# A gather of 32 per loop turn shared between GpSimd and SyncE in a graph-network kernel on one Trainium2 core

## The chip, the cores and the metric

The kernel runs on one core of one Trainium2 chip. Its time is the device time of one execution in microseconds (us). Before the change it is 2132.71 us, the median of three runs (2131.5 to 2132.8).

The engines are TensorE (PE, with its weight loads as PEld), VectorE (DVE), ScalarE (ACT), GpSimd (POOL) and SyncE (SP). SP computes nothing here: it waits on semaphores and issues DMA transfers. POOL issues the gathers, that is, DMA transfers whose source rows are named by a list of indices.

## The reference

A layer of a graph network with 6250 nodes and 206250 edges, sorted by destination. Each node has 160 values: 64 scalars and 32 vectors of three.

```python
h = jnp.maximum(_layernorm(x, axis=-1), 0.0)
# inside the layer, with node_input = h:
h = relu(edge_length_embedded @ W_fc1 * (1/sqrt(10))) * RELU_GAIN
w = h @ W_fc2 * (1/sqrt(100))                    # weights of each edge
l0, l1 = _fctp_scalar_attr(x0, x1, a, W_l1_0, W_l1_1)
y0 = l0[edge_src]; y1 = l1[edge_src]             # the gather
m0 = w0 * y0 * e0
m1 = (w1 * y0)[:, :, None] * e1[:, None, :]
m2 = (w2 * e0)[:, :, None] * y1
m3 = w3 * einsum('eud,ed->eu', y1, e1) * INV_SQRT3
s0..s3 = segment_sum(m0..m3, edge_dst)           # sum over the edges of a node
out = si + 0.5 * (products of s0..s3 with W_l2_*)
x = x + out
```

## The kernel before, in words

**Node stage (0 to some 80 us).** The nodes are normalized and multiplied by the first weights, and SP stores the result as `table` in HBM, one row of 160 float32 (640 bytes) for each node (line 239).

**Edge stage (86 to some 2120 us).** The edges are cut into 403 groups of T = 4 tiles of P = 128 edges. Per group:

- POOL gathers 128 rows of `table` for each of the four tiles into a row buffer `y[:, j]` (line 361), so 4 gathers a group and 1612 in all. There are G = 4 row buffers. Before it writes one it waits until DVE has finished with the group that used it four groups ago (`msg_done`, line 357).
- PE computes the hidden values of the edges (`fc1`, L823), ACT takes the relu (L459), and PE computes the edge weights (`fc2`, L830).
- DVE makes the one-hot matrix `hot` (L647), waits for the group's rows (line 650), multiplies the vectors by the attributes (`dots`, L620), scales `hot` (L654), sums the dots (L624), and makes the messages from rows and weights (L630, L635, L640). L640 is the last of a group's messages: it brings `msg_done` to 4 per group.
- PE sums the messages over the edges of each destination (`windows`, L858 and L860), and DVE adds the result into `acc` (L682).

The hardware loop runs over pairs of turns, that is 8 groups or 32 gathers; there are 50 pairs (`PAIRS`) and 3 groups after them. In each pair one block of 128 nodes is finished besides (PE L836 to L848, DVE L667), and its rows are stored by SP (line 254).

**What SP does in the edge stage.** `load_half` (lines 263 to 277) loads, for every two groups, the radial inputs `rad` (10 x 1024, waits for `fc1_done`, line 266), the indices `idx` (128 x 8, waits until the gathers that used the old ones have landed, line 271), and the attributes `attr_sb` (128 x 32, waits for `msg_done`, line 275). That is 12 transfers in a pair, issued strictly one after another: what stands behind a wait on SP waits too. A transfer whose address is in a register needs small register instructions ahead of it (FUSED_REGOPS or ALU_OP, and MOVE), which the trace shows on the queue of SP.

Nothing but these semaphores orders POOL, SP, DVE, ACT and PE against each other.

Of the kernel before, what the change touches and what calls it, by code (L numbers as in the profile page):

```python
# [6 lines left out]
P = 128  # L7
N = 6250
E = 206250
MUL0, MUL1 = 64, 32  # L10
C = MUL0 + 3 * MUL1
# [3 lines left out]
CHUNK = 7  # L15
CHUNKS = BLOCKS // CHUNK
assert CHUNKS % 2
STORES = CHUNKS + 1
# [6 lines left out]
NP = BLOCKS * P  # L25
# [12 lines left out]
assert TURNS == 2 * PAIRS + 1  # L38
LAG = 3

IN_LOOP = PAIRS - LAG
# [22 lines left out]

def gnn_layer(nc, x, src, dst, radial, attr, avec, w_lin, w_lin_z, w_self, w_self_z, w_last, wf1, wf2, out):
    ctx = ExitStack()
    with ctx:
        def sb(name, shape, dt=F32):
            return ctx.enter_context(nc.sbuf_tensor(name, shape, dt))

        def sem(name):
            return ctx.enter_context(nc.semaphore(name))
# [61 lines left out]
        idx_sum = sb("idx_sum", [P, 1], I32)  # L134
        rows_in = y[:, 0, :, :].rearrange("p t c -> p (t c)")[:, 0:4 * P]

# [37 lines left out]
        ld_rad = [sem(f"ld_rad{c}") for c in range(2)]  # L174
        gathered = [sem(f"gathered{j}") for j in range(G)]
        fc1_done = sem("fc1_done")
# [43 lines left out]
        def _(sp):  # L220
# [41 lines left out]

            def load_half(i, c, first):
                k = i * 2 + c
                if not first:
                    sp.wait_ge(fc1_done, (k - 1) * HALF)
                    sp.sem_inc(sp_passed, 1)
                sp.dma_start(rad[:, c, :], radial[:, bass.ds(k * HALF * GE, HALF * GE)]).then_inc(ld_rad[c], 16)
# [4 lines left out]
                sp.dma_start(idx[:, c, :], src[:, bass.ds(k * HALF * T, HALF * T)]).then_inc(ld_idx[c], 16)  # L273
# [3 lines left out]
                sp.dma_start(attr_sb[:, c, :, :], attr[:, bass.ds(k * HALF * T, HALF * T), :]).then_inc(ld_attr[c], 16)  # L277

            def windowed():
                for c in range(2):  # L280
                    load_half(0, c, True)

                half_way = TURNS // 2
                with sp.Fori(1, half_way) as i:
                    for c in range(2):
                        load_half(i, c, False)
                early = (half_way // 2 - LAG - 1) // CHUNK
                for c in range(early):
                    store_out(c, 0, CHUNK)
                with sp.Fori(half_way, TURNS) as i:  # L290
                    for c in range(2):
                        load_half(i, c, False)
                store_rest(early)

            def general():

                sp.wait_ge(zeroed, 1)
                with sp.Fori(0, ND // P) as b:
                    sp.dma_start(sums_d[bass.ds(b * P, P), :], acc[:, 0, 0:4 * P]).then_inc(g_zeroed, 16)
                with sp.Fori(0, GROUPS) as g:  # L300
                    sp.wait_ge(g_free, g + 1)
                    sp.sem_inc(sp_passed, 1)
                    sp.dma_start(rad[:, 0, 0:GE], radial[:, bass.ds(g * GE, GE)]).then_inc(g_loaded, 16)
                    sp.dma_start(idx[:, 0, 0:T], src[:, bass.ds(g * T, T)]).then_inc(g_loaded, 16)
                    sp.dma_start(attr_sb[:, 0, 0:T, :], attr[:, bass.ds(g * T, T), :]).then_inc(g_loaded, 16)
                sp.wait_ge(g_turn, TILES + 1)
                with sp.Fori(0, BLOCKS) as b:
                    sp.wait_ge(g_block_free, b + 1)
                    sp.sem_inc(sp_passed, 1)
                    sp.dma_start(rows_in, sums_d[bass.ds(b * P, P), :]).then_inc(g_block_in, 16)  # L310
                store_rest(0)
# [6 lines left out]
        def _(pool):  # L318
# [33 lines left out]

            def gather_group(i, j, first):
                if j % HALF == 0:
                    pool.wait_ge(ld_idx[j // HALF], i * 16 + 16)
                if not first:
                    pool.wait_ge(msg_done, (i * G + j - G + 1) * 4)
                    pool.sem_inc(pool_passed, 1)
                for t in range(T):
                    col = (j % HALF) * T + t  # L360
                    nc.gpsimd.indirect_dma_start(  # L361
                        out=y[:, j, t, :], out_offset=None, in_=table,
                        in_offset=bass.IndirectOffsetOnAxis(ap=idx[:, j // HALF, col:col + 1], axis=0),
                    ).then_inc(gathered[j], 16)

            def windowed():
                for j in range(G):
                    gather_group(0, j, True)
                with pool.Fori(1, TURNS - 1) as i:  # L369
                    for j in range(G):  # L370
                        gather_group(i, j, False)

                for j in range(LEFT):
                    gather_group(TURNS - 1, j, False)

# [141 lines left out]
        def _(dve):  # L517
# [96 lines left out]

            def attr_of(j, a, b):
                return attr_sb[:, j // HALF, (j % HALF) * T:(j % HALF) * T + T, a:b]

            def edge_dots(j):

                nc.vector.tensor_tensor(dots[:, :, :, :], vectors(j), attr_of(j, 1, 4).unsqueeze(3).to_broadcast([P, T, 3, MUL1]),  # L620
                                        ALU.mult).then_inc(dots_done, 1)
# [19 lines left out]

            def messages(i, j):
                g, s = i * G + j, j % 2
                if j % HALF == 0:
                    dve.wait_ge(ld_attr[j // HALF], i * 16 + 16)
# [4 lines left out]
                dve.wait_ge(gathered[j], i * (16 * T) + 16 * T)  # L650
                edge_dots(j)
                dve.wait_ge(hot_done, g + 1)

                nc.vector.tensor_tensor(hot[:, s, :, 1:V, :], hot[:, s, :, 0:1, :].to_broadcast([P, T, 4, W]),  # L654
                                        attr_of(j, 0, 4).unsqueeze(3).to_broadcast([P, T, 4, W]), ALU.mult).then_inc(msg_done, 1)
                dve.wait_ge(dots_done, g + 1)
                sum_dots()
                dve.wait_ge(fc2_done, g + 1)
                scalar_products(j, s)
                vector_products(j, s)  # L660
                dve.wait_ge(dot_done, g + 1)
                dot_products(s)
# [24 lines left out]
            def windowed():  # L687
                def pair(k, first, last_of_block):
                    for j in range(2 * G):
                        g = k * (2 * G) + j  # L690
                        messages(k * 2 + j // G, j % G)
# [9 lines left out]
                for j in range(LEFT):  # L701
                    g = (TURNS - 1) * G + j
                    messages(TURNS - 1, j)
                    accumulate(g - 1, (g - 1) % 2, base_of(g - 1), False)
# [6 lines left out]
            def general():  # L711
# [4 lines left out]
                with dve.Fori(0, GROUPS) as g:  # L716
                    dve.wait_ge(g_loaded, g * 48 + 48)
                    dve.wait_ge(g_rows, g * (16 * T) + 16 * T)
                    edge_dots(0)
                    dve.drain()  # L720
# [50 lines left out]
        def _(pe):  # L771
# [130 lines left out]
            def general():  # L902
# [15 lines left out]
                with pe.Fori(0, BLOCKS) as b:  # L918
                    pe.wait_ge(g_block_in, b * 16 + 16)
                    for v in range(4):  # L920
                        ins = nc.tensor.transpose(ps_w[:, 0, v, 0:P], rows_in[:, v * P:(v + 1) * P], ident[:, :])
                    ins.then_inc(g_block_turned, 1)
# [71 lines left out]
```

## Time and profile before

| | |
|---|---|
| median of three runs | 2132.71 us (2131.5 to 2132.8) |
| the profiled execution | 2139.31 us |
| its span, first to last instruction | 2137.5 us |
| mean granted TensorE clock | 0.928 of full speed |
| busy shares | PE 95%, PEld 75%, DVE 79%, POOL 74%, ACT 16% |
| gathers | 1612, first at 86.0 us, last at 2117.7 us |
| DMA | 158.29 MB, 74 GB/s over the span |

Busy means that an instruction runs; a gather's busy time is POOL's time to issue it, not the time that the data takes. "Idle before" is time in which an engine had nothing running, and the releaser is what ended it; "issue" is idle time in which it waited for nothing that the profile shows. Names with a q (SPq, DVEq) are the instruction queues of the engines. The profiled execution is 6.6 us longer than the median.

### The profile page before, as it was taken

How to read it: one execution, taken by the hardware profiler on the slowest of the kernel's cores; microseconds unless marked ns; L12 is line 12 of the kernel's file. 1: busy time of each engine (PE TensorE's matmuls, PEld its weight loads, DVE VectorE, ACT ScalarE, POOL GpSimd, SP SyncE). 2: the span in 40 equal slices, each digit the busy share in tenths (PEclk: the TensorE clock that was granted, in tenths of full speed). 3: DMA queues.
4: the chain of work that ended last, by engine and by line, in shares of the span. 5: the costliest groups of instructions: out<-in, count | busy, mean ns of one | idle time of the engine just before them, and what ended most of it. 6: DMA issues, size and time to landing. Idle time of an engine off the chain costs nothing.

```text
span 2137.5 us, 42022 instructions
## 1 busy us (share of the span) xinstructions
PE 2021.8 (95%) x11466; PEld 1603.7 (75%) x11466; DVE 1684.6 (79%) x4634; ACT 343.0 (16%) x636; POOL 1576.3 (74%) x1637
## 2 busy tenths in 40 slices
PE   6899999999999999999999999999999999999998
PEld 5677777787778778777777777777777777777776
DVE  6478878788787888888877888887888878888786
ACT  4311111111111111111111111111111111111111
POOL 6277777777777777777777777777777777777774
PEclk8699999899998998999998989999999989998998
DMA  4223222223222332232232223233232322322233
GB/s 134 72 70 72 72 72 70 71 71 72 71 72 69 71 72 71 70 73 71 71 103 71 71 71 71 72 71 72 71 71 71 73 70 70 73 72 69 71 72 91
DMA packets 159932, 158.29 MB, mean 74 GB/s; under 512 B 86882, under 2 KB 131846, under 8 KB 159914
## 3 DMA queue, kind: packets, MB, share of 16 engines
q0 software_dynamic: 77376, 132.16, 25.0%
q1 hardware_dynamic: 81400, 24.49, 5.2%
q10 hardware_dynamic: 1138, 1.43, 0.2%
q8 instruction: 8, 0.13, 0.0%
q14 instruction: 10, 0.08, 0.0%
HBM read 149.90 MB, written 8.03 MB: 74 GB/s over the span
## 4 chain that ended last, share of the span: by engine, by line
POOL 31%; issue 25%; DMA 18%; DVE 15%; PE 9%; DVEq 1%; POOLq 1%; ACT 0%; SPq 0%; ACTq 0%
POOL y L361 31%; DMA y<-table,idx 17%; DVE hot L654 5%; DVE msg L630 5%; DVE dot L624 4%; PE ps_s L858 2%; PE ps_w L830 2%; PE ps_s L860 2%; PE ps_h L823 1%; DVE dots L620 1%; PE ps_w L792 1%; DVE stats L520 1%; PE ps_h L781 0%; POOLq L369 0%; DVEq L685 0%
## 5 line engine op out<-in xcount | busy, mean ns | idle before, releaser
L361 POOL DMA_INDIRECT y<-table,idx x1612 | 1541.9, 957 | 536.5 <-issue 490.5
L830 PEld LDWEIGHTS ps_w<-w_fc,hr 100*128 100x128 f32 x3224 | 539.3, 197 | 331.8 <-issue 331.8
L830 PE MATMUL ps_w<-w_fc,hr 100*128 100x192 f32 x3224 | 663.0, 351 | 0.0
L858 PE MATMUL ps_s<-hot,msg 128*128 128x128 f32 x3224 | 485.0, 298 | 67.9 <-DVE msg L640 67.3
L858 PEld LDWEIGHTS ps_s<-hot,msg 128*128 128x128 f32 x3224 | 436.6, 206 | 112.3 <-DVE msg L640 109.0
L459 ACT ACTIVATE hr<-ps_h 100x512 f32<-100x512 f32 x403 | 240.7, 597 | 1681.1 <-PE ps_h L823 1681.1
L823 PE MATMUL ps_h<-rad,w_fc 10*100 10x512 f32 x806 | 464.1, 656 | 5.7 <-DMA rad<-in_radial 5.7
L620 DVE TENSOR_TENSOR dots<-y,attr_sb 128x384 f32<-128x384 f32 x403 | 225.1, 559 | 276.7 <-DMA y<-table,idx 276.3
L860 PE MATMUL ps_s<-hot,msg 128*128 128x64 f32 x3224 | 432.0, 280 | 0.0
L860 PEld LDWEIGHTS ps_s<-hot,msg 128*128 128x128 f32 x3224 | 423.3, 205 | 0.0
L682 DVE TENSOR_TENSOR acc<-acc,ps_s 64x32 f32 (+1 forms) x1612 | 325.2, 202 | 71.6 <-PE ps_s L860 31.1
L630 DVE TENSOR_TENSOR msg<-ps_w,y 128x512 f32<-128x512 f32 x403 | 278.4, 691 | 21.1 <-PE ps_w L830 8.6
L654 DVE TENSOR_TENSOR hot<-hot,attr_sb 128x512 f32<-128x512 f32 x403 | 275.3, 683 | 0.0
L624 DVE TENSOR_REDUCE dot<-dots 128x128 f32<-128x384 f32 x403 | 235.8, 585 | 0.0
L635 DVE TENSOR_TENSOR msg<-ps_w,y 128x384 f32<-128x384 f32 x403 | 220.3, 547 | 0.0
L647 DVE TENSOR_TENSOR hot<-iota_w,dst_rel 128x128 f32<-128x128 f32 x403 | 117.8, 292 | 19.1 <-DMA attr_sb<-in_attr 6.2
L823 PEld LDWEIGHTS ps_h<-rad,w_fc 10*100 10x100 f32 x806 | 103.1, 166 | 35.5 <-DMA rad<-in_radial 5.8
L640 DVE TENSOR_TENSOR msg<-ps_w,dot 128x128 f32<-128x128 f32 x403 | 112.7, 280 | 0.0
L421 ACT ACTIVATE hid<-xres,shift,rstd 128x160 f32 (+1 forms) x98 | 47.9, 510 | 3.7 <-DVE shift L535 3.7
L781 PE MATMUL ps_h<-ident,hid 128*128 128x128 f32 x49 | 19.1, 396 | 23.9 <-ACT hid L421 23.9
L667 DVE SCALAR_TENSOR_TENSOR xres<-ps_s,a_sb,xres 128x160 f32 x47 | 17.7, 377 | 24.5 <-PE ps_s L860 24.1
L842 PE MATMUL ps_s<-w_out,fin_in 128*128 128x160 f32 x94 | 25.0, 350 | 12.8 <-DVE msg L640 12.8
(79 smaller groups left out, 527.0 us busy)
## 6 DMA issues: line engine op xcount, KB each, us to landing
y<-table,idx POOLq DMA_INDIRECT x1612
rad<-in_radial SPq DMA_DIRECT2D x202, 40.0 KB
xres<-in_x SPq DMA_DIRECT2D x7, 560.0 KB, 4.2
table<-y SPq DMA_DIRECT2D x6, 560.0 KB, 3.2
out<-xres SPq DMA_DIRECT2D x6, 560.0 KB, 4.7
idx<-in_src SPq DMA_DIRECT2D x202, 4.0 KB
attr_sb<-in_attr SPq DMA_DIRECT2D x202, 16.0 KB
dst_i<-in_dst ACTq DMA_DIRECT2D x1, 808.0 KB, 6.3
```

What stands on the lines that cost most here:

```text
L361: nc.gpsimd.indirect_dma_start(out=y[:, j, t, :], out_offset=None, in_=table, in_offset=bass.IndirectOffsetOnAxis(ap=idx[:, j // HALF, col ...
L459: nc.scalar.activation(hr[:, s, :], ps_h[0:N_RADIAL, s, 0:GE], ACT.Relu, scale=K_RADIAL).then_inc(relu_done, 1)
L620: nc.vector.tensor_tensor(dots[:, :, :, :], vectors(j), attr_of(j, 1, 4).unsqueeze(3).to_broadcast([P, T, 3, MUL1]), ALU.mult).then_inc(do ...
L624: nc.vector.tensor_reduce(dot[:, :, :], dots[:, :, :, :].rearrange("p t d u -> p t u d"), AX.X, ALU.add).then_inc(dot_done, 1)
L630: nc.vector.tensor_tensor(msg[:, s, :, 0:2 * MUL0].rearrange("p t (k u) -> p t k u", k=2), ps_w[:, s, :, 0:2 * MUL0].rearrange("p t (k u) ...
L635: nc.vector.tensor_tensor(msg[:, s, :, 2 * MUL0:M - MUL1].rearrange("p t (d u) -> p t d u", d=3), ps_w[:, s, :, 2 * MUL0:NW - MUL1].unsque ...
L654: nc.vector.tensor_tensor(hot[:, s, :, 1:V, :], hot[:, s, :, 0:1, :].to_broadcast([P, T, 4, W]), attr_of(j, 0, 4).unsqueeze(3).to_broadcas ...
L682: nc.vector.tensor_tensor(to, to, p[rows, cols].rearrange("p (v n) -> p v n", n=W), ALU.add).then_inc(acc_done, 1)
L823: nc.tensor.matmul(ps_h[0:N_RADIAL, j % 2, 0:GE], w_fc1[:, :], rad[:, j // HALF, (j % HALF) * GE:(j % HALF + 1) * GE], start=True, stop=Tr ...
L830: ins = nc.tensor.matmul(ps_w[:, s, t, 0:NW], hr[:, s, t * P:(t + 1) * P], w_fc2[:, :], start=True, stop=True)
L858: nc.tensor.matmul(ps_s[:, s, 0:4 * W], msg[:, s, t, 0:P], hot[:, s, t, 1:V, :], start=(t == 0), stop=(t == T - 1))
L860: ins = nc.tensor.matmul(ps_s[:, s, 4 * W:6 * W], msg[:, s, t, P:M], hot[:, s, t, 0:2, :], start=(t == 0), stop=(t == T - 1))
```

## The change

Of the 32 gathers of a pair, the last (group 7 of the pair, tile 3) is shared. POOL gathers its first 64 rows only. The other 64 rows are fetched by SP, one transfer of 640 bytes for each, whose source address comes from a register. SP first loads the 64 indices into one partition (`idx_row`, one transfer in a pair, from a copy of `src` in another layout), and loads registers from there in four batches of 16.

A fifth row buffer is added: group 7 of a pair uses buffer 4, so groups 3 and 7 now have a buffer each that is used once in a pair. Indices and attributes are loaded for four groups at once instead of two (4 transfers in a pair instead of 8), the radial inputs as before (4). SP's order of work in a pair is written out by hand in `step`. The rows of group 7 may be written once DVE has finished all groups of the pair before (`msg_done` at k times 32), and DVE waits for four more semaphores (`rows_in`) at group 7.

```diff
+ROWS = 64
+BATCH = 16
+BATCHES = ROWS // BATCH
+APART = 2 * G - 1
+
+def slot_of(p, j):
+    return G if p * G + j == APART else j
...
-        idx = sb("idx", [P, 2, HALF * T], I32)
-        attr_sb = sb("attr_sb", [P, 2, HALF * T, 4])
+        idx = sb("idx", [P, 2, G * T], I32)
+        attr_sb = sb("attr_sb", [P, 2, G * T, 4])
-        y = sb("y", [P, G, T, C])
+        y = sb("y", [P, G + 1, T, C])
+        idx_row = sb("idx_row", [1, ROWS], I32)
...
+            def load_idx(k, p, first):
+                i = k * 2 + p
                 if not first:
-                    for j in range(HALF * c, HALF * c + HALF):
-                        sp.wait_ge(gathered[j], i * (16 * T))
+                    for j in range(G):
+                        sp.wait_ge(gathered[p * G + j], k * (16 * T))
                     sp.sem_inc(sp_passed, 1)
+                sp.dma_start(idx[:, p, :], src[:, bass.ds(i * G * T, G * T)]).then_inc(ld_idx[p], 16)
+
+            def load_attr(k, p, first):
+                i = k * 2 + p
                 if not first:
-                    sp.wait_ge(msg_done, (k - 1) * HALF * 4)
+                    sp.wait_ge(msg_done, (i - 1) * (4 * G))
...
+            def load_row_idx(k):
+                tile = k * (2 * G * T) + 2 * G * T - 1
+                sp.dma_start(idx_row[:, :], src_row[bass.ds(tile, 1), P - ROWS:P]).then_inc(ld_row, 16)
+
+            def fetch_rows(k, q):
+                _, nodes = nc.values_load_multi_w_load_instructions(
+                    idx_row[0:1, q * BATCH:(q + 1) * BATCH], engines=[sp.engine], min_val=0, max_val=NP - 1, ...)
+                for r, node in enumerate(nodes):
+                    at = P - ROWS + q * BATCH + r
+                    sp.dma_start(y[at:at + 1, G, T - 1, :], table[bass.ds(node, 1), :]).then_inc(rows_in[q], 16)
+
+            def step(k, first):
+                load_idx(k, 1, first)
+                sp.wait_ge(ld_row, k * 16 + 16)
+                if not first:
+                    sp.wait_ge(msg_done, k * (8 * G))
+                    sp.sem_inc(sp_passed, 1)
+                fetch_rows(k, 0)
+                load_attr(k, 1, first)
+                load_rad(k * 2 + 1, 0, False)
+                fetch_rows(k, 1)
+                load_rad(k * 2 + 1, 1, False)
+                load_idx(k + 1, 0, False)
+                fetch_rows(k, 2)
+                load_attr(k + 1, 0, False)
+                load_rad(k * 2 + 2, 0, False)
+                fetch_rows(k, 3)
+                load_rad(k * 2 + 2, 1, False)
...
+                def steps(lo, hi):
+                    with sp.Fori(lo, hi) as k:
+                        load_row_idx(k)
+                        step(k, False)
...
+            def gather_group(k, p, j, first):
+                if j == 0:
+                    pool.wait_ge(ld_idx[p], k * 16 + 16)
+                n = p * G + j
                 if not first:
-                    pool.wait_ge(msg_done, (i * G + j - G + 1) * 4)
+                    held = 2 * G if n in (G - 1, APART) else G
+                    pool.wait_ge(msg_done, (k * (2 * G) + n - held + 1) * 4)
                     pool.sem_inc(pool_passed, 1)
                 for t in range(T):
+                    rows = P - ROWS if n == APART and t == T - 1 else P
                     nc.gpsimd.indirect_dma_start(
-                        out=y[:, j, t, :], ...
+                        out=y[0:rows, slot_of(p, j), t, :], ...
                     ).then_inc(gathered[n], 16)
...
+                n, at = p * G + j, slot_of(p, j)
+                dve.wait_ge(gathered[n], k * (16 * T) + 16 * T)
+                if n == APART:
+                    for q in range(BATCHES):
+                        dve.wait_ge(rows_in[q], k * (16 * BATCH) + 16 * BATCH)
+                edge_dots(p, j)
```

The lines that are not shown rename variables and pass the pair and its half instead of the turn.

## Rows read from the trace of the kernel before

**Rows 1.** The page, part 1: busy time of each engine.
```profile
PE 2021.8 (95%) x11466; PEld 1603.7 (75%) x11466; DVE 1684.6 (79%) x4634; ACT 343.0 (16%) x636; POOL 1576.3 (74%) x1637
```

**Rows 2.** One line, the gathers (L361): nanoseconds least/median/most; idle by releaser.
```profile
L361 POOL DMA_INDIRECT y<-table,idx x1612: 942/946/1456, 86.0 to 2117.7; - x180
...
  issue: 490.5, 1461
  DVE msg L630: 43.9, 144
...
  DVE dots L620: 276.3, 338
```

**Rows 3.** Timeline, 2085 to 2091 us: start, length, engine, line, operation.
```profile
2085.14 0.95 POOL L361 DMA_INDIRECT y<-table,idx  x1 [0.30 <-issue]
2085.23 0.56 DVE L620 TENSOR_TENSOR dots<-y,attr_sb 128x384 f32<-128x384 f32 x1 [0.77 <-DMA y<-table,idx]
...
2086.39 0.95 POOL L361 DMA_INDIRECT y<-table,idx  x1 [0.30 <-issue]
...
2088.00 0.28 DVE L640 TENSOR_TENSOR msg<-ps_w,dot 128x128 f32<-128x128 f32 x1
...
2090.31 0.56 DVE L620 TENSOR_TENSOR dots<-y,attr_sb 128x384 f32<-128x384 f32 x1 [0.89 <-DMA y<-table,idx]
```

**Rows 4.** Busy time of engines by stretch; then clock, DMA share, GB/s.
```profile
300.00:1000.00 700.00, 675.11 (x3831) 533.04 (x3830) 565.62 (x1546) 105.82 (x191) 530.96 (x556) 0.93 0.30 71
1080.00:1090.00 10.00, 10.00 (x39) 8.33 (x37) 5.62 (x15) 0.60 (x1) 7.56 (x8) 0.52 0.83 243
```

**Rows 5.** Timeline, 1080 to 1094 us, with a low clock.
```profile
1080.24 2.48 SPq L254 DMA_DIRECT2D out<-xres  x3
...
1083.14 1.21 SPq L268 DMA_DIRECT2D rad<-in_radial  x1
...
1088.99 0.56 DVE L620 TENSOR_TENSOR dots<-y,attr_sb 128x384 f32<-128x384 f32 x1 [2.99 <-DMA y<-table,idx]
```

**Rows 6.** Waits of the queue of SP: total us, times, longest.
```profile
SPq L272 <- DMA y<-table,idx: 1056.2, 200, 10.3
SPq L276 <- DVE msg L640: 543.8, 200, 6.4
```

**Rows 7.** Lines 268, 273, 277 on SP (three answers): nanoseconds least/median/most.
```profile
L268 SPq DMA_DIRECT2D rad<-in_radial x202: 312/312/1208, 80.9 to 2099.1; - x101
L268 SPq FUSED_REGOPS  x200: 52/58/71, 86.7 to 2098.9; - x100
...
L273 SPq DMA_DIRECT2D idx<-in_src x202: 347/352/377, 81.4 to 2105.5; - x101
...
L277 SPq DMA_DIRECT2D attr_sb<-in_attr x202: 332/333/433, 81.8 to 2108.6; - x101
```

**Rows 8.** Line 277 on SP: what runs in 1009.36 to 1009.37 us.
```profile
L277 SPq ALU_OP  x1: 33/33/33, 1009.4 to 1009.4; - x1
```

**Rows 9.** Timeline on SP, 1009.4 to 1010.0 us.
```profile
1009.49 0.33 SPq L277 DMA_DIRECT2D attr_sb<-in_attr  x1
```

**Rows 10.** Timeline on SP, 81 to 84 us: transfers back to back.
```profile
81.37 0.38 SPq L273 DMA_DIRECT2D idx<-in_src  x1
81.78 0.42 SPq L277 DMA_DIRECT2D attr_sb<-in_attr  x1
...
82.66 0.35 SPq L273 DMA_DIRECT2D idx<-in_src  x1
```

**Rows 11.** Loads of registers: line 685 (DVE), line 211 (SP).
```profile
L685 DVEq TENSOR_LOAD <-base_i x403: 299/305/1010, 99.2 to 2128.2; - x135
...
L211 SPq TENSOR_LOAD <-flag_i x1: 477/477/477, 79.6 to 79.6; - x1
```

**Rows 12.** The chain that ended last, 80 to 90 us: start, length, what.
```profile
81.37 1.69 DMA idx<-in_src
```

More of the change, by code:

```diff
@@ L134, in gnn_layer @@
         idx_sum = sb("idx_sum", [P, 1], I32)
-        rows_in = y[:, 0, :, :].rearrange("p t c -> p (t c)")[:, 0:4 * P]
+        sums_in = y[:, 0, :, :].rearrange("p t c -> p (t c)")[:, 0:4 * P]
         def ps(name, shape):
@@ L174, in gnn_layer @@
         ld_rad = [sem(f"ld_rad{c}") for c in range(2)]
-        gathered = [sem(f"gathered{j}") for j in range(G)]
+        gathered = [sem(f"gathered{j}") for j in range(2 * G)]
+        ld_row = sem("ld_row")
+        rows_in = [sem(f"rows_in{q}") for q in range(BATCHES)]
         fc1_done = sem("fc1_done")
@@ new lines, in load_row_idx @@
+            def load_row_idx(k):
[3 more added lines that the diff above has]
+                _, nodes = nc.values_load_multi_w_load_instructions(
+                    idx_row[0:1, q * BATCH:(q + 1) * BATCH], engines=[sp.engine], min_val=0, max_val=NP - 1,
+                    skip_runtime_bounds_check_because="src names rows of x, as in the reference's own gather")
+                for r, node in enumerate(nodes):
+                    at = P - ROWS + q * BATCH + r
+                    sp.dma_start(y[at:at + 1, G, T - 1, :], table[bass.ds(node, 1), :]).then_inc(rows_in[q], 16)
@@ L279, in windowed @@
             def windowed():
+                load_idx(0, 0, True)
+                load_row_idx(0)
+                load_attr(0, 0, True)
                 for c in range(2):
[L281 to L287, printed above, removed]
+                    load_rad(0, c, True)
+                sp.wait_ge(table_out, 16 * STORES)
@@ L288, in windowed @@
+                step(0, True)
+                half_way = PAIRS // 2
+                def steps(lo, hi):
+                    with sp.Fori(lo, hi) as k:
+                        load_row_idx(k)
+                        step(k, False)
+                steps(1, half_way)
+                early = (half_way - LAG - 1) // CHUNK
                 for c in range(early):
                     store_out(c, 0, CHUNK)
-                with sp.Fori(half_way, TURNS) as i:
-                    for c in range(2):
-                        load_half(i, c, False)
+                steps(half_way, PAIRS)
@@ L351, in _ @@
             pool.wait_ge(table_out, 16 * STORES)
-            def gather_group(i, j, first):
-                if j % HALF == 0:
-                    pool.wait_ge(ld_idx[j // HALF], i * 16 + 16)
+            def gather_group(k, p, j, first):
+                if j == 0:
+                    pool.wait_ge(ld_idx[p], k * 16 + 16)
+                n = p * G + j
                 if not first:
-                    pool.wait_ge(msg_done, (i * G + j - G + 1) * 4)
+                    held = 2 * G if n in (G - 1, APART) else G
+                    pool.wait_ge(msg_done, (k * (2 * G) + n - held + 1) * 4)
                     pool.sem_inc(pool_passed, 1)
                 for t in range(T):
-                    col = (j % HALF) * T + t
+                    rows = P - ROWS if n == APART and t == T - 1 else P
                     nc.gpsimd.indirect_dma_start(
-                        out=y[:, j, t, :], out_offset=None, in_=table,
-                        in_offset=bass.IndirectOffsetOnAxis(ap=idx[:, j // HALF, col:col + 1], axis=0),
-                    ).then_inc(gathered[j], 16)
+                        out=y[0:rows, slot_of(p, j), t, :], out_offset=None, in_=table,
+                        in_offset=bass.IndirectOffsetOnAxis(ap=idx[0:rows, p, j * T + t:j * T + t + 1], axis=0),
+                    ).then_inc(gathered[n], 16)
             def windowed():
-                for j in range(G):
-                    gather_group(0, j, True)
-                with pool.Fori(1, TURNS - 1) as i:
+                for p in range(2):
                     for j in range(G):
-                        gather_group(i, j, False)
+                        gather_group(0, p, j, p == 0 or j == G - 1)
+                with pool.Fori(1, PAIRS) as k:
+                    for p in range(2):
+                        for j in range(G):
+                            gather_group(k, p, j, False)
                 for j in range(LEFT):
-                    gather_group(TURNS - 1, j, False)
+                    gather_group(PAIRS, 0, j, False)
             def general():
@@ L690, in pair @@
                         g = k * (2 * G) + j
-                        messages(k * 2 + j // G, j % G)
+                        messages(k, j // G, j % G)
                         if j >= 1 or not first:
@@ L702, in windowed @@
                     g = (TURNS - 1) * G + j
-                    messages(TURNS - 1, j)
+                    messages(PAIRS, 0, j)
                     accumulate(g - 1, (g - 1) % 2, base_of(g - 1), False)
```

43 lines of the change are left out of this document (21 added, 22 removed).

## The prediction

> **What bounds the kernel now.** I read the busy shares first. PE looks like the bound at 95% and POOL has 74% [rows 1], but a busy share doesn't say who waits. So the next view is the line of the gathers: POOL issues 1612 of them between 86.0 and 2117.7 us, each 0.946 us long, and the idle time before them is "issue", 490.5 us in 1461 cases, or 0.34 us each with the start left in; the 144 cases put down to DVE come to 43.9 us, 0.30 us each [rows 2]. The timeline shows the same 0.30 us before gathers that waited for nothing, so those 144 are no waits either [rows 3]. POOL is therefore never held up: it starts one gather every 1.25 us, 2085.14 to 2086.39 [rows 3], and on average every (2117.7 - 86.0) / 1611 = 1.261 us [rows 2]. A pair of 32 gathers takes 40.36 us, and 50 pairs are nearly the whole span. DVE waits for gathered rows 338 times, 276.3 us in all [rows 2], and its groups start 5.08 us apart [rows 3].
>
> PE is the bound only for short stretches. The mean clock is 0.93, and in 1080 to 1090 us it is 0.52 [rows 4], close to the lower level of 1.2 GHz, after a stretch in which PE had small gaps. DVE starts its next group late there, 2.99 us idle [rows 5], but POOL stays at 7.56 us busy in those 10 us, the same share as elsewhere [rows 4]: the row buffers cover it. So less time on POOL shortens the whole, if what replaces it fits beside.
>
> **What the change removes.** 50 times, half of one gather. With 128 rows it costs 0.946 us [rows 2]. No gather with fewer rows is in the trace. The bounds: nothing saved (all fixed cost), and half, 0.473 us (all by row). A negative value has no reason, as POOL does the same with fewer rows. The only row there is gives the cost with all rows and shows no fixed part except the 0.30 us between gathers, which stays; I take three quarters of the upper end, 0.355 us, an estimate. Saved: 50 x 0.355 = 17.7 us, ends 0 and 23.7. POOL's pair becomes 40.0 us.
>
> The Trainium skill (DMA: Bandwidth & Descriptors, Anatomy of one DMA) says of descriptor generation that "You can emit a lot of descriptors before the incremental cost shows up". By that sentence the saving is 0 and the sum is 2132.7; no row here shows it either way.
>
> **What it adds on SP.** 64 transfers of one row in a pair. SP issues one after another, so this is a sum. Nearest row for a transfer with a register address: line 277 starts its first register instruction by 1009.36 [rows 8], its transfer at 1009.49 for 0.33 us [rows 9], and back to back there are about 0.045 us until the next (81.37 + 0.38 is followed at 81.78, with 0.03 us) [rows 10]. That is 0.13 + 0.33 + 0.045 = 0.505 us. The transfer itself takes 0.352 and 0.333 us with 128 rows and 0.312 with 10 [rows 7]; with one row I take 0.30, an estimate on that slope, so 0.475 us for each. Upper end: 0.352 plus 0.145 and 0.045, 0.542. Lower end: 0.30 with register instructions that overlap half, 0.41. Transfers behind a large one take longer (0.42 us for attributes behind indices), behind a small one not (0.35 for indices behind the radial load) [rows 10]; rows are small. Registers: four loads of 16. One load of one value takes 0.305 us on DVE and 0.477 on SP [rows 11]; if a batch is one load, 1.2 to 1.9 us in a pair. If each register were its own load, 64 x 0.305 = 19.5 us: bound of the unknown.
>
> **The chain that these form.** The rows of a pair may be fetched only when DVE is done with the pair before, and DVE can't end group 7 before they have landed. One turn of this circle: register loads 1.2; rows 64 x 0.475 = 30.4; six other transfers that `step` puts between the fetches (two of attributes, three radial, one of indices) at 0.6 each with semaphores and register work (0.505 and some 0.1), 3.6; landing of the last row, 1.69 - 0.38 = 1.3 as for the indices [rows 10, 12]; and DVE's group from L620 to the end of L640, 2085.23 to 2088.28, 3.05 [rows 3]. Sum 39.55 us, against 40.0 for POOL. It fits by 0.45 us. The point at which it binds is (40.0 - 9.15) / 64 = 0.482 us a row; the point at which it is no better than before is (40.36 - 9.15) / 64 = 0.488.
>
> **What has cover.** SP has the room now: it waits 1056 us for gathers and 544 us for messages [rows 6]. Indices for the next half turn are issued some 18 us into the chain and needed by POOL near 34; attributes are issued at 27 and needed at 40; the radial load of the next pair's first groups is issued at 27 and needed by PE near 32, the thinnest cover of the three. Four transfers fewer in a pair save SP 2.4 us, one more costs 0.6. The wait on `msg_done` holds what is queued behind it on SP, but only POOL, PE and DVE's next loads stand there. The fifth buffer costs nothing; it gives SP 36 us to fill it. The four waits on `rows_in` cost DVE nothing if the rows are there. Three stores of 560 KB in the middle hold SP for 2.48 us, and the transfer behind them takes 1.21 us [rows 5]; with 0.45 us of room in a pair that is 2 us once, and it delays group 7 of one pair. A low clock starts the chain late too when it falls at a pair's end: the 2.99 us idle [rows 5] is 2.2 above the usual 0.77 [rows 3]; earlier in a pair DVE makes it up. I count 2 us for all of this.
>
> The Trainium skill (DMA: Bandwidth & Descriptors, Issuing engines are not separate DMA queues) speaks against the change: transfers of all engines end on the same 16 DMA engines, so spreading them "will only save the time on the sequencer". Here exactly that time is the bound: the DMA engines are busy 0.30 and POOL never waits [rows 2, 4]. By the rule's first half nothing is gained, 2132.7; by the rows 2117.
>
> Sum: 2132.7 - 17.7 + 2 = 2117.0 us. The profiled execution is 6.6 us above the median (2139.3, span 2137.5); the terms are differences, and I set them against the median. What a measurement of this kernel can tell from no change is about 0.2%, 4.3 us.
>
> **Rivals.**
>
> *SP's chain becomes the bound* (slower). Place: `fetch_rows` between `msg_done` of group 7 and `rows_in` of the next. It decides from 0.482 us a row on, and 0.01 us above costs 0.64 us a pair, 32 us in all. With 0.51 us a row (the measured 0.505) and 0.477 for a register load: 32.6 + 1.9 + 3.6 + 1.3 + 3.05 = 42.5 us, 2.1 over the present 40.36, times 49: 2236 us. With the upper end 0.542 it is 2339; with 0.49, about 2140. For it: the nearest row is over the threshold, and POOL would be held where it now runs free. Against it: one row is less than 128, and the durations fall with the rows. With a register load for each value it would be over 3000 us. Chance 0.36.
>
> *A half gather costs POOL what a whole one costs* (no change). The chain fits, POOL's pair stays 40.36 us: 2132.7 less 0 to 4. For it: 0.946 us for 128 rows could be mostly start and end. This is where the skill's sentence above leads. Chance 0.12.
>
> *The change does what it says and PE is next.* At full clock PE needs about 36 us a pair (95% of 40.36 with the slow stretches inside); it would have to exceed 40.0, and isn't near. Its price would be the gain alone. It is inside the forecast.
>
> **Numbers.** Forecast 0.52, chain 0.36, fixed cost 0.12. These give faster 0.52, same 0.12, slower 0.36. The forecast's own range is 2107 (0.473 saved, and no 2 us) to 2128. For 8 in 10 the range must take in half or more of the chain's case: 2107 to 2240.
>
> **What the next profile shows.** Right: 50 gathers well under 0.95 us, near 0.6; POOL still idle by "issue" alone; SP with waits left in each pair at the `msg_done` line; DVE's dots of group 7 released by a gather, not by a row transfer. Wrong: POOL idle with DVE as releaser for several us in each pair, dots waiting for `table` rows issued by SP, a row every 0.49 us or more on the queue of SP, and a pair longer than 40.4 us. The second rival shows as 50 gathers of 0.9 us.

## The result, and the profile after

The changed kernel takes 2148.34 us (median of four runs, 2146.71 to 2151.22) beside 2132.11 us for the kernel before on the same chip: ratio 1.0064, 95% interval 1.0041 to 1.0086. It is slower by 0.6%, where 0.7% faster was forecast. The profiled execution took 2149.61 us, its span is 2147.8 us, the mean granted clock 0.923. The medians differ by 16.2 us, the spans of the two traces only by 10.3, since the execution profiled before was 6.6 us above its median and this one 1.3. What follows explains the traces; some 4 us of the difference between the medians are in none of it.

The busy shares of the page, part 1, beside [rows 1]:

```profile
PE 2028.5 (94%) x11466; PEld 1609.2 (75%) x11466; DVE 1684.2 (78%) x4634; ACT 342.8 (16%) x636; POOL 1588.6 (74%) x1637
```

PE, DVE and ACT are as before. POOL is busy 12 us longer, though it has less to gather. The line of the gathers (columns as in [rows 2]):

```profile
L420 POOL DMA_INDIRECT y<-table,idx x1612: 899/947/1475, 84.2 to 2128.4; - x180
...
  issue: 522.2, 1571
  DVE hot L720: 8.8, 29
...
  DVE dots L681: 226.9, 270
```

POOL's idle time is still "issue" in gaps of 0.30 us: from the first gather to the last the idle time between them adds up to 491.2 us, against 490.7 before. So POOL is still never held up, and still sets the pace; but from the first gather's start to the last it takes 2128.4 - 84.2 = 2044.2 us, where [rows 2] give 2031.7. The 12.5 us are in the gathers themselves. Before, 51 of the 1612 took over 1.0 us; now 100 do. What they take above 0.946 us adds up to 17.3 us before and 30.4 us after: 13.1 us more. The least of the line, 899 ns, is the half gather: 50 of them, 0.899 to 0.907 us, so each saves some 0.045 us and all of them 2.3 us. 13.1 - 2.3 = 10.8 of the 12.5 us; another 1.5 us is the ordinary gather, 947 ns in the median instead of 946, 1500 times.

SP's new work: the loads of registers and the instructions of one row, each with least, median and most in nanoseconds:

```profile
L303 SPq TENSOR_LOAD <-idx_row x200: 1132/1214/1257, 81.3 to 2106.7; - x100
...
L308 SPq FUSED_REGOPS  x3200: 37/37/52, 82.5 to 2114.2; - x189
L308 SPq MOVE y<-table x3200: 29/29/37, 82.6 to 2114.3; - x189
L308 SPq DMA_DIRECT2D y<-table x3200: 224/228/279, 82.7 to 2114.3; - x189
```

A row starts every 0.412 us in the median (16 of them take 6.44 us in the timeline below), and a batch of 16 registers is one instruction of 1.21 us. The waits that these cause (total us, times, longest):

```profile
DVE dots L681 <- DMA y<-table,idx: 226.9, 270, 9.0
...
DVE dots L681 <- DMA y<-table: 47.6, 35, 4.8
...
SPq L316 <- DVE msg L701: 116.0, 48, 5.4
...
SPq L287 <- DMA y<-table,idx: 7.8, 2, 6.1
```

DVE waits for gathered rows less than before (226.9 us against 276.3) and, new, for SP's rows: 35 times in 50 pairs, 47.6 us. Only 13 of the 35 waits are long (1.8 to 4.8 us); the other 22 last 0.3 to 1.1 us, about as long as the usual wait for a gather (0.8 us). SP waits 48 times, 2.4 us each, for DVE's last message of the pair (L316), at the start of its rows, and has almost no wait for gathers left (L287; 1056 us in [rows 6]). So the circle is closed nearly all the time: SP begins when DVE lets it, and DVE gets the last rows when it wants them or a little later. One turn of it, in the timeline (start, length, engine, line):

```profile
536.39 0.28 DVE L701 TENSOR_TENSOR msg<-ps_w,dot 128x128 f32<-128x128 f32 x1
...
566.05 6.44 SPq L308 DMA_DIRECT2D y<-table  x16
...
566.85 0.56 DVE L681 TENSOR_TENSOR dots<-y,attr_sb 128x384 f32<-128x384 f32 x1 [0.70 <-DMA y<-table,idx]
...
573.57 0.56 DVE L681 TENSOR_TENSOR dots<-y,attr_sb 128x384 f32<-128x384 f32 x1 [1.98 <-DMA y<-table]
...
574.04 0.68 DVE L720 TENSOR_TENSOR hot<-hot,attr_sb 128x512 f32<-128x512 f32 x1
...
574.25 1.30 POOL L420 DMA_INDIRECT y<-table,idx  x1 [0.30 <-issue]
...
577.67 0.55 DVE L681 TENSOR_TENSOR dots<-y,attr_sb 128x384 f32<-128x384 f32 x1
...
578.13 0.68 DVE L720 TENSOR_TENSOR hot<-hot,attr_sb 128x512 f32<-128x512 f32 x1
578.35 1.29 POOL L420 DMA_INDIRECT y<-table,idx  x1 [0.30 <-issue]
```

Group 7 of this pair should start near 572 us; its last rows are issued until 572.5, and DVE starts at 573.57 after 1.98 us without work. Then it is behind, finds the rows of the next group there, and starts the next group after 4.10 us instead of 5.08 [rows 3]. Its scaling of `hot` (L720) now falls right ahead of two gathers (574.04 and 574.25, 578.13 and 578.35), and these take 1.30 and 1.29 us instead of 0.95. Another pair, the same view:

```profile
1098.93 0.56 DVE L681 TENSOR_TENSOR dots<-y,attr_sb 128x384 f32<-128x384 f32 x1 [2.33 <-DMA y<-table]
...
1099.41 0.68 DVE L720 TENSOR_TENSOR hot<-hot,attr_sb 128x512 f32<-128x512 f32 x1
1099.50 1.41 POOL L420 DMA_INDIRECT y<-table,idx  x1 [0.30 <-issue]
...
1104.92 0.68 DVE L720 TENSOR_TENSOR hot<-hot,attr_sb 128x512 f32<-128x512 f32 x1
1104.96 1.48 POOL L420 DMA_INDIRECT y<-table,idx  x1 [0.30 <-issue]
...
1109.03 0.68 DVE L720 TENSOR_TENSOR hot<-hot,attr_sb 128x512 f32<-128x512 f32 x1
1109.25 1.28 POOL L420 DMA_INDIRECT y<-table,idx  x1 [0.30 <-issue]
```

Here 2.33 us of waiting, and three long gathers: 1.41, 1.48 and 1.28 us. They start 0.09, 0.04 and 0.22 us after L720 starts, and all end 1.50 to 1.52 us after its start: wherever in the scaling they begin, it is as if the gather began about 0.55 us into it, and then took its 0.95 us. Over the whole of both traces, a gather that starts 0 to 0.4 us after the start of this scaling is long (over 1.0 us) in 34 of 34 cases before and 76 of 78 after. The number of such meetings is what has changed.

Why it has changed can be counted from the waits. When DVE waits for a gather, it starts `dots` some 0.1 us after POOL has begun another gather, and `hot` 0.47 us after `dots`; the scaling is then over just when POOL's next gather begins, 1.25 us after the last one (2085.14, 2085.23 and 2086.39 in [rows 3]). When DVE waits for nothing, or for a row of SP, nothing holds the two in step. The table counts DVE's 403 groups by what `dots` waited for, and the long gathers that begin in each kind of group, from 0.15 us before its `dots` to 0.15 us before the next one (in each trace one more begins ahead of the first group):

| trace | groups that waited for a gather | long gathers beside them | all other groups | long gathers beside them |
|---|---|---|---|---|
| before | 338 | 2 | 65 | 48 |
| changed | 270 | 10 | 133, 35 of them for SP's row | 89 |

In the changed kernel these other groups come in 63 stretches. The 28 stretches without a wait for a row hold 39 long gathers, where the 27 of before held 48. The 35 stretches with such a wait, 34 of which begin with it, hold 50: that is the whole surplus. 36 of the 50 belong to the 13 long waits. POOL itself is never stopped: no idle time between two of its gathers is over 0.32 us, so neither DVE nor PE and its clock hold it up in the edge stage.

### The profile page after: what moved, and what is told of

It reads as the page before. It is cut to its first block, busy times and chain, and to the rows that moved or that the text cites. A ratio compares the mean times of both kernels' runs of the same rounds, so it can differ in the third digit from the quotient of the medians.

```text
span 2147.8 us, 51135 instructions
## 1 busy us (share of the span) xinstructions
PE 2028.5 (94%) x11466; PEld 1609.2 (75%) x11466; DVE 1684.2 (78%) x4634; ACT 342.8 (16%) x636; POOL 1588.6 (74%) x1637
## 4 chain that ended last, share of the span: by engine, by line
POOL 42%; issue 31%; SPq 9%; PE 8%; DMA 5%; DVE 4%; DVEq 1%; POOLq 0%; ACT 0%; ACTq 0%
POOL y L420 42%; SPq L308 6%; DMA y<-table,idx 4%; PE ps_w L896 2%; SPq L303 2%; PE ps_s L924 1%; DVE hot L720 1%; PE ps_s L926 1%; PE ps_h L889 1%; PE ps_w L858 1%; DVE stats L581 1%; DVEq L751 1%; DVE dot L685 0%; DMA table<-y 0%; SPq L281 0%
## 5 line engine op out<-in xcount | busy, mean ns | idle before, releaser
L896 PEld LDWEIGHTS ps_w<-w_fc,hr 100*128 100x128 f32 x3224 | 544.8, 199 | 334.2 <-issue 334.2
L681 DVE TENSOR_TENSOR dots<-y,attr_sb 128x384 f32<-128x384 f32 x403 | 225.0, 558 | 274.9 <-DMA y<-table,idx 226.9
L748 DVE TENSOR_TENSOR acc<-acc,ps_s 64x32 f32 (+1 forms) x1612 | 325.7, 202 | 81.6 <-PE ps_s L926 40.5
L720 DVE TENSOR_TENSOR hot<-hot,attr_sb 128x512 f32<-128x512 f32 x403 | 275.5, 684 | 0.0
L889 PEld LDWEIGHTS ps_h<-rad,w_fc 10*100 10x100 f32 x806 | 103.6, 166 | 39.9 <-DMA rad<-in_radial 10.6
```

What stands on the lines that cost most here:

```text
L681: nc.vector.tensor_tensor(dots[:, :, :, :], vectors(slot_of(p, j)), attr_of(p, j, 1, 4).unsqueeze(3).to_broadcast([P, T, 3, MUL1]), ALU.mu ...
L748: nc.vector.tensor_tensor(to, to, p[rows, cols].rearrange("p (v n) -> p v n", n=W), ALU.add).then_inc(acc_done, 1)
L889: nc.tensor.matmul(ps_h[0:N_RADIAL, j % 2, 0:GE], w_fc1[:, :], rad[:, j // HALF, (j % HALF) * GE:(j % HALF + 1) * GE], start=True, stop=Tr ...
L896: ins = nc.tensor.matmul(ps_w[:, s, t, 0:NW], hr[:, s, t * P:(t + 1) * P], w_fc2[:, :], start=True, stop=True)
```

## The experiments

**Theories.** *Late rows*: the half gather saves next to nothing; the rows land late in many pairs, DVE's catching up shifts its `hot` scaling onto the starts of gathers, and POOL loses 13 us there. *SP's traffic*: 3200 small transfers slow the gathers by themselves. *The sides*: fewer and larger loads of indices and attributes, the fifth buffer and the new waits cost the time.

**Two kinds of chip.** On some chips the median of the kernel before itself was 2838 to 2920 us instead of 2132 to 2137, and no run of it there was under 2808. There the engines show gaps between instructions for which they waited for nothing (ACT has 502.7 us of them in the trace of the half gather alone, 5.7 us in the trace of before), and the granted clock is 0.68 to 0.79. The numbers are therefore given by the kind of chip, and no run is compared with one on the other kind. Why these chips are so was not found.

### Three kernels on a chip on which the kernel before takes 2134.49 us

The changed kernel itself was not run again on this chip: its 0.6% stand on four runs on the chip of the result.

**The rows fetched, but to a place that nobody reads.** The half gather stays, the 64 transfers a pair stay, DVE doesn't wait for them (SP does, before it fetches the next ones). This leaves out 64 rows of one tile in each pair.

```diff
-sp.dma_start(y[at:at + 1, G, T - 1, :], table[...]).then_inc(rows_in[q], 16)
+sp.dma_start(aside[at:at + 1, :], table[...]).then_inc(rows_in[q], 16)
...
-if n == APART:
-    for q in range(BATCHES):
-        dve.wait_ge(rows_in[q], ...)
```

> As e3_aside, now beside a kernel before of 2135 us. Theory A (late rows): VectorE never waits for them, some 50 gathers over 1 us, 2131 us. Rival C (the 3200 transfers and SyncE's register work slow GpSimd by themselves): 2147 us, 100 long gathers.

Measured 2135.47 us, 1.0002 [0.9983, 1.0022]. The line of the gathers:

```profile
L428 POOL DMA_INDIRECT y<-table,idx x1612: 899/946/1447, 80.7 to 2111.8; - x180
...
  DVE dots L689: 290.1, 354
```

All of SP's transfers, no loss: 56 gathers over 1.0 us, 18.6 us above 0.946, near the 17.3 of before; DVE waits for no row. SP's traffic isn't the cause. From the first to the last gather it takes 2031.2 us, 0.5 less than before: 2.3 saved, 1.3 lost again to long gathers, the rest to slightly longer gaps. So the half gather's worth, even with all rows out of DVE's way, can't be measured.

**The side edits alone.** POOL gathers all rows; no rows on SP, no registers, no waits of DVE for them; the larger loads and the fifth buffer stay.

```diff
-    rows = P - ROWS if n == APART and t == T - 1 else P
+    rows = P
...
-    fetch_rows(k, 0)
...
```

> As e5_sides, now beside a kernel before of 2135 us. Theory A (late rows cause the loss): within 4 us of the kernel before, some 50 gathers over 1 us. Rival B (loads for four groups and the new order cause it): 12 us or more slower.

Measured 2133.98 us, 0.9997 [0.9978, 1.0016]:

```profile
L413 POOL DMA_INDIRECT y<-table,idx x1612: 942/946/1452, 80.4 to 2111.3; - x180
...
  DVE dots L674: 270.6, 333
```

56 long gathers (17.0 us), 2030.9 us from first to last. The sides cost nothing that can be measured, and bring nothing.

**48 rows instead of 64.** One batch less on SP, 80 rows on POOL, the whole computation.

```diff
-ROWS = 64
+ROWS = 48
...
-                fetch_rows(k, 3)
```

> As e4_rows48, now beside a kernel before of 2135 us. Theory A (late rows): no waits of VectorE on rows, some 50 gathers over 1 us, 2132 us. Rival C (traffic by count): three quarters of the loss stay, 12 us slower than before.

Measured 2129.71 us, 0.9971 [0.9954, 0.9988]: 0.3% faster than the kernel before, and the best version here that computes everything. Gathers, then waits of SP's queue:

```profile
L419 POOL DMA_INDIRECT y<-table,idx x1612: 897/946/1456, 81.0 to 2107.4; - x180
...
  DVE dots L680: 282.5, 347
...
SPq L287 <- DMA y<-table,idx: 305.7, 50, 7.5
SPq L316 <- DVE msg L700: 137.9, 49, 5.1
```

SP ends its rows some 8 us earlier (16 x 0.412 and one register load of 1.21): it now waits at all 50 turns for the gathers (L287), where it waited twice. DVE has no wait for a row left in the whole trace. 48 long gathers (14.2 us); 2026.4 us from first to last, 5.3 less than before: 2.4 from the 50 shorter gathers (0.897 us) and 3.1 from fewer long ones. That part isn't shown to come from the edit, as the traces without late rows differ by as much among themselves (48 to 56 long gathers, 14.2 to 18.6 us). Both edits that take the lateness away, this one and `aside`, take the loss away, and this one leaves nothing out. The same count as above, for these three:

| trace | groups that waited for a gather | long gathers beside them | all other groups | long gathers beside them |
|---|---|---|---|---|
| aside | 354 | 20 | 49 | 35 |
| sides | 333 | 7 | 70 | 48 |
| 48 rows | 347 | 7 | 56 | 40 |

### A whole gather left out, on a chip with 2136.61 us before

To see what POOL's time is worth: the side edits alone, and the last gather of each pair not done (128 rows of a tile left out).

> e5_sides with the last gather of a pair left out altogether (128 rows of one tile in 32 stay zero). Theory A: GpSimd is the pace and a whole gather costs 1.25 us of it (0.946 and 0.30 between two), so 50 x 1.25 = 62 us less than the kernel before: 2070 us where that takes 2132; PE becomes the pace where its clock is low, so it may stop at 2090. If GpSimd is not the pace: no gain.

Measured 2083.77 us in two runs, 0.9753 [0.9704, 0.9801], 52.8 us less (43 to 63 by the interval):

```profile
L421 POOL DMA_INDIRECT y<-table,idx x1562: 942/946/1473, 81.4 to 2066.8; - x196
...
  issue: 507.6, 1534
```

50 gathers less at 0.946 + 0.30 would be 62.3 us; from first to last it is 1985.5 us against 2030.9 with the sides alone (on the other chip), 45.4 less. The rest is lost to long gathers, as in the change: 96 of them, 33.6 us above 0.946, 16.6 more than with the sides alone (62.3 - 16.6 = 45.7). POOL has no gap over 0.31 us here, so PE doesn't become the pace. DVE didn't wait for a gather in 141 groups, and 90 of the long gathers are beside these, without one transfer of a row. So a change in the rhythm of DVE against POOL is enough for the loss, whatever brings it. Leaving out a gather is worth 0.9 to 1.1 us each; leaving out half of one shortens it by 0.05.

### The slower chips

**The half gather alone**, on the kernel before (64 rows left out in each pair):

```diff
+rows = P // 2 if odd and j == G - 1 and t == T - 1 else P
-out=y[:, j, t, :], ... ap=idx[:, ...]
+out=y[0:rows, j, t, :], ... ap=idx[0:rows, ...]
```

> The kernel before with the last gather of every second turn cut to its first 64 rows; the other 64 rows of that tile are left out. Theory A (a gather costs almost the same with half the rows: 0.899 against 0.946 us in the profile of the changed kernel): 50 gathers at 0.90 us, 2.3 us saved, 2130 us. My forecast's term (0.355 us each): 2114 us. Fully by row (0.473 us each): 2109 us.

Measured 2832.54 beside 2838.51 us, 0.9992 [0.9957, 1.0027]. The same kernel on two more such chips:

> The same kernel as e1_half, since the kernel before took 2838 us beside that run instead of 2132, with engines waiting for their instructions. Beside a kernel before of 2132 us: theory A (a gather costs almost the same with half the rows): 50 gathers at 0.90 us, 2.3 us saved, 2130 us. My forecast's term: 2114 us.

> As e1_half, now beside a kernel before of 2135 us: 50 gathers at 0.90 us, 2.3 us less than before, inside what the measurement can tell. My forecast's term: 18 us less.

Measured 2838.41 beside 2840.95 us, 0.9994 [0.9957, 1.0031], and 2935.47 beside 2920.54 us, 1.0072 [1.0019, 1.0126], so the ratio scatters by more than the 0.1% in question. The line of the gathers, and the longest of the idle times before them:

```profile
L362 POOL DMA_INDIRECT y<-table,idx x1612: 899/946/1471, 79.8 to 2811.8; - x180
...
  DVE msg L644: 616.5, 139
```

The duration of the half gather is a reading: 899 ns. The times say nothing of it, since POOL is held by DVE for 616.5 us here.

**The other three versions on the first of these chips**:

> The changed kernel with whole gathers on GpSimd and no transfers of rows: only the loads for four groups, SyncE's new order and the fifth buffer are left. Theory A (late rows cause the loss): like the kernel before, 2132 us within 4, and some 50 gathers over 1 us. Rival B (the loads for four groups and the new order cause it): 2145 us or more.

> The changed kernel, with SyncE's rows written to a tile that nobody reads, and no wait of VectorE on them (64 rows of one tile in 32 are left out of the result, zeros or old values stand there). Theory A (late rows): VectorE is never late for them, gathers over 1 us fall from 100 to some 50, time 2130 us. Rival C (the 3200 transfers and SyncE's register work slow GpSimd by themselves, whoever waits): 2145 us, 100 long gathers.

> 48 rows by SyncE instead of 64, 80 by GpSimd. Theory A (late rows): SyncE's turn is shorter by 16 x 0.41 + 1.2 = 7.8 us, the rows are there before VectorE asks, long gathers some 50, time 2131 us. Rival C (traffic by count): three quarters of the loss stay, 2143 us. By the chain alone, as in my second case: no wait on rows at all.

Measured beside 2838.51 us: sides 2953.23 (1.0411 [1.0359, 1.0464]), aside 3186.91 (1.1245 [1.1191, 1.13]), 48 rows 3059.46 (1.0783 [1.0728, 1.0837]). The same three on another such chip:

> The same kernel as e5_sides (loads for four groups, new order and fifth buffer alone). Theory A (late rows cause the loss): 2132 us within 4, some 50 gathers over 1 us. Rival B (the loads and the order cause it): 2145 us or more.

> The same kernel as e3_aside (rows to a tile that nobody reads, VectorE doesn't wait for them; 64 rows of one tile in 32 left out). Theory A (late rows): some 50 gathers over 1 us, 2130 us. Rival C (the 3200 transfers and SyncE's register work slow GpSimd by themselves): 2145 us, 100 long gathers.

> The same kernel as e4_rows48. Theory A (late rows): SyncE's turn is shorter by 7.8 us, no waits of VectorE on rows, some 50 gathers over 1 us, 2131 us. Rival C (traffic by count): 2143 us.

Measured beside 2840.95 us: 2948.73 (1.037 [1.03, 1.0441]), 3197.34 (1.1234 [1.115, 1.1318]) and 3061.3 (1.0753 [1.0675, 1.0831]). All three expectations failed, and no theory of mine for 2132 us explains such losses. `aside` has 64 rows a pair and no wait of DVE for them, and loses 12%. Its trace shows SP itself as the bound: a row starts every 0.73 us on the average instead of 0.42, so the 64 rows of a pair last 56.5 us instead of 34.6, SP waits for DVE only 4 times at the start of its rows (17.3 us), and PE waits 558 us for the radial inputs that stand behind rows in SP's queue. That doesn't explain `sides`, which has no rows and fewer loads than the kernel before and still loses 4%; its cause was not found. None of it bears on the result, so the three were then run on the chip above.

**The dose**, on such chips again: the changed kernel, the same with one load moved behind the last rows (`load_attr(k + 1, 0)` after `fetch_rows(k, 3)`), and 80 rows in five batches.

> The changed kernel again, on the chip of these runs: 1.006 of the kernel before, some 100 gathers over 1 us, VectorE waits 48 us for rows.

> The changed kernel with one load of attributes moved from ahead of the last batch of rows to behind it, so that the rows land some 0.65 us earlier; nothing else. Theory A (late rows): VectorE's waits on rows fall from 47.6 us to under 25, long gathers from 100 towards 60, 2138 us, 10 less than the changed kernel. Rival D (something else in it that goes with 64 rows): no change, 2148 us.

> 80 rows by SyncE, 48 by GpSimd. The circle of the forecast with measured terms: now 4 x 1.21 + 64 x 0.411 + six others + landing = 36.9 us from the wait to the dots of group 7, and 3.05 of VectorE, 40.0 in all. 16 rows and one batch load more are 7.8 us: 47.8 us a pair, 7.5 over 40.3, times 49 = 365 us, 2500 us, VectorE waits for rows in each pair and GpSimd for VectorE. If GpSimd stayed the pace (lateness taken up by the buffers) 2150 us.

None of these came true, as the kernel before took 2920.54 us there. Measured beside it: changed kernel 3311.63 (1.1338 [1.1256, 1.1421]), moved load 3264.22 (1.1186 [1.1112, 1.126]), 80 rows 3727.93 (1.2785 [1.2677, 1.2893]). Both doses once more, on one more chip:

> As r64_order, for a chip on which the kernel before takes some 2135 us. Theory A (late rows): rows some 0.65 us earlier, VectorE's waits on rows under 25 us instead of 47.6, long gathers from 100 towards 60, 1.001 of the kernel before instead of 1.006. Rival D (something else that goes with 64 rows): 1.006.

> As r80, for a chip on which the kernel before takes some 2135 us. The circle with its measured terms, 36.9 + 3.05 us, and 7.8 more: 47.8 us a pair, 2500 us, GpSimd waits for VectorE. If the buffers took up the lateness: 2150 us.

Measured beside 2912.49 us: moved load 3271.5 (1.1246 [1.115, 1.1342]), 80 rows 3725.98 (1.2823 [1.2682, 1.2963]). Waits of the changed kernel (total us, times, longest):

```profile
POOL y L420 <- DVE msg L701: 1085.0, 157, 18.0
...
DVE dots L681 <- DMA y<-table: 437.9, 47, 14.9
```

and with 80 rows:

```profile
POOL y L421 <- DVE msg L702: 1519.3, 154, 25.1
...
DVE dots L682 <- DMA y<-table: 727.9, 50, 22.3
```

Here the first rival is what happens: late rows in nearly every pair, and POOL held by DVE. A pair takes 64.0 us with 64 rows and 72.1 us with 80: 8.1 us more for 16 rows and a register load, where SP's rows of a pair last 8.4 us longer on the average (58.5 and 66.8 us from the first to the last). Where the circle binds, what is added to it is added to the pair. The moved load gives 47 us, 1.0 us a pair. But `aside` loses nearly as much without any wait for rows, so what these chips show is SP's slowness more than the lateness. On a chip with 2132 us the dose was not measured.

## Why the prediction was wrong, point by point

Two steps failed: the saving of 17.7 us, which was 2.3, and the statement that the circle fits with 2 us for all stalls. It doesn't fit, and DVE's catching up cost POOL 13.1 us in long gathers, a cost that stood in no term. With the ordinary gathers' 1.5 us these give 2132.7 - 2.3 + 13.1 + 1.5 = 2145 us; the 3 us that remain to the measured 2148.3 are not assigned. That the measured time lies inside 2107 to 2240 is luck: the range was stretched for a chain that holds POOL up, and POOL was never held up.

**The saving, 17.7 us: the larger of the two.** "All rows and no fixed part shown, so three quarters of half": 0.355 us a gather. Measured 0.045 us, 2.3 us in all. A gather's 0.946 us is almost all fixed: 0.90 us with 64 rows and with 80. With this term at 2.3 us there was nothing to pay for any loss. The second rival held this mechanism, with a chance of 0.12; its time, 2128.7 to 2132.7 us, was missed too, since it also let the chain fit. The sentence of the Trainium skill (DMA: Bandwidth & Descriptors, Anatomy of one DMA) that many descriptors come before the incremental cost shows was right for it, and the trace agrees with it (0.045 us less for 64 rows less). 0 would have been the better choice between the ends 0 and 23.7: a row that shows only one size says nothing of the slope.

**The circle, 39.55 us: nearly right, by luck, from errors that cancel.** Rows at 0.412 us instead of 0.475, 64 of them: -4.0 us. Register loads at 4 x 1.21 instead of 4 x 0.305: +3.6 us, since a load of 16 values takes SP 1.21 us where a load of one takes 0.477 [rows 11]; the number of instructions was right, their length was not. The six other transfers take some 4.2 us instead of 3.6. Measured in the pair of the timeline above: DVE's last message ends at 536.67, group 7 starts at 573.57, DVE's group is 3.05 us: 39.9 us. Over the 35 pairs with a wait for a row the median is 40.1 us.

**"It fits by 0.45 us": it doesn't fit.** Forecast were 39.55 against 40.0 us; measured are 40.1 us for the circle (39.9 to 40.5 in all but two of the 35 pairs) against 40.36 - 0.05 = 40.3 us for POOL on the average. That leaves 0.2 us, and not even these in a quiet pair: the 40.36 us already hold 0.35 us of long gathers (17.3 us in 50 pairs), and a pair without any takes POOL 32 x (0.946 + 0.305) - 0.05 = 40.0 us. So the last rows come about when DVE wants them or a little later, and every small delay makes DVE late: it waited for them in 35 pairs of 50, in 13 of them for 1.8 to 4.8 us. The prediction counted 2 us for all of this and compared two means. The stall that it named is in the trace, in the pair at half time: SP issues its first row 5.6 us after DVE's message instead of 1.4, and DVE waits 4.8 us.

**The rival of the chain: half right.** Rows were late, as it said; but POOL was never held, as its price of 2236 us needs. DVE made up its waits before the row buffers ran out. The price came by a road that neither case had: a late DVE that catches up starts its `hot` scaling at other moments of POOL's gathers. Both traces before and after have the cause in plain sight, and [rows 2] show 1456 ns as the most beside a median of 946. I read the median and never asked when a gather takes 1.46 us. Only the late rows, not SP's transfers and not the sides, bring more of these in this change: the surplus of 50 is in the 35 stretches with a wait for a row, `aside` and `sides` keep 56 long gathers and the time of before, and 48 rows have 48 and gain.

**What was right.** PE isn't the bound; the sides cost nothing; SP itself has room left, 2.4 us in a pair at the `msg_done` line; POOL's gaps stay at 0.30 us. DVE's `dots` released by rows of `table` was named as a sign of being wrong, and came.

**The rule on issuing engines.** The Trainium skill (same page, Issuing engines are not separate DMA queues) holds that only the time on the sequencer is saved, which is usually small beside the transfer. The whole gather left out shows that POOL's time isn't small here, 52.8 us for 50. What made the rule right in the end is that half a gather hands over half of the rows and a twentieth of the time.

**Still open.** The changed kernel beside `aside`, `sides` and 48 rows on one chip; the dose (80 rows, moved load) on a chip with 2132 us; a late DVE produced without any row transfers there; some 3 us of the loss; and what makes the other chips slow.

## What to carry to other kernels

Before work is split, find what part of an instruction's time goes with its size: here leaving out a gather gains 1 us and halving it 0.05. Don't trust a circle that fits by 1% of its length on paper: set it against the pace of the undisturbed engine, not against a mean that holds its disturbances, and leave it the spread from pair to pair as slack (48 rows had 8 us, and won 0.3% where 64 rows lost 0.6%, on another chip). Where a bound engine shows a most far above its median, ask what ran beside those cases: a change elsewhere can move the phase and make them more.

## What the runs showed of the hardware

Some instructions of DVE hold up a gather on POOL. Gathers that start in the first 0.4 us of the `hot` scaling (128x512) or of `dots` (128x384), which both read two operands from SBUF, take up to 1.48 us instead of 0.95. The long ones end at a fixed time after DVE's instruction began: 1.50 us after the start of the scaling, 1.37 us after the start of `dots`. Those that start 0 to 0.2 us before `dots` aren't longer (none above 1.0 us of 335 in the trace of before), and of those that start during a message, which reads one operand from PSUM (401), or during the reduction (333) none is either. SP's transfers of a row stay at 224 to 279 ns throughout the trace after. The Trainium skill (SBUF — State Buffer, SBUF: two separate sides) describes such an exclusive lock for a DVE instruction with two SBUF inputs against a GpSimd instruction that reads SBUF, and for a gather that starts second the trace agrees: the gather reads its indices there. The page says the same of a DVE instruction that starts second; that isn't seen here, as the 335 `dots` that start 0 to 0.2 us after a gather take 0.558 us in the median, and 48 later ones 0.551.

A transfer of one row of 640 bytes costs SP 0.228 us, and 0.412 us from start to start with its address from a register (median; on the slower chips 0.71 us in the mean against 0.42 here); 128 rows cost 0.33 to 0.35 us [rows 7]. A load of 16 registers costs 1.21 us, of one 0.477 [rows 11].
